# A gated attention block on one core: the first batch's second FFN matrix quantised in four pieces between the RELU low halves

## The reference, cut to what matters

```python
xn  = layernorm(x)
q, k, v = (gelu(xn @ W1n + b1n) @ W2n + b2n for n in "qkv")
s   = tril(q @ k.T / sqrt(C * T)) @ v          # scores times mask, no softmax
s   = layernorm(s) * ln_w + ln_b

def quantize(W):                                # to -1, 0, 1
    gamma = mean(abs(W))
    return clip(round(W / (gamma + 1e-5)), -1, 1)
h   = relu(xn @ quantize(W1).T + b1)            # 512 x 1024 for a batch
g   = silu(h @ quantize(W2).T + b2)
out = x + s * g
```

## Time and profile before

| | |
|---|---|
| median of the timed runs | 321.74 us |
| the profiled execution's own time | 322.64 us |
| its span | 320.8 us |
| mean granted PE clock | 0.983 |
| PE busy | 307.9 us (96%) |
| DVE busy | 242.2 us (75%) |
| ACT busy | 230.1 us (72%) |
| POOL busy | 129.8 us (40%) |

### The profile page before, as it was taken

How to read it: one execution, slowest core, us unless ns; L and a number is a source line. 1 busy time by engine, 2 the same in 40 slices (tenths; PEclk the granted TensorE clock), 3 DMA queues, 4 the chain that set the end, 5 groups by cost and what they waited for, 6 DMA issues and landing times.

```text
span 320.8 us, 5759 instructions
## 1 busy us (share of the span) xinstructions
PE 307.9 (96%) x1850; PEld 274.5 (86%) x1850; DVE 242.2 (75%) x556; ACT 230.1 (72%) x424; POOL 129.8 (40%) x106
## 2 busy tenths in 40 slices
PE   5998599999999999999999999999999999999993
PEld 5885499888998899888998899988998889988993
DVE  3589967797768887597787887597777977677677
ACT  1799553899549983799549984699648985599642
POOL 2015462526253542718245342817334362610223
PEclk9899599999999999999999999999999999999999
DMA  7943351320003100140003100050003200010001
GB/s 243 379 125 108 134 145 51 109 90 0 3 0 131 65 0 0 54 143 0 0 0 131 66 0 0 2 169 26 0 0 128 69 0 0 0 65 3 0 2 66
DMA packets 15771, 20.10 MB, mean 63 GB/s; under 512 B 1936, under 2 KB 12688, under 8 KB 15760
## 3 DMA queue, kind: packets, MB, share of 16 engines
q1 hardware_dynamic: 15056, 19.04, 17.7%
q10 hardware_dynamic: 704, 0.93, 0.8%
HBM read 15.74 MB, written 4.22 MB: 62 GB/s over the span
## 4 chain that ended last, share of the span: by engine, by line
PE 87%; DVE 5%; ACT 4%; DMA 2%; issue 1%; SPq 0%; DVEq 0%; ACTq 0%
PE bank L714 87%; DMA raw_qkv<-in_W2k 2%; ACT bank L367 1%; ACT g_hi L366 1%; DVE w2q L503 1%; DVE gw L584 1%; ACT r_lo L333 1%; DVE s L500 0%; DVE s_lo L614 0%; DVE x_stats L454 0%; ACT L366 0%; ACT o_square L340 0%; DVE s L604 0%; DVE x_all L639 0%; PE bank L699 0%
## 5 line engine op out<-in xcount | busy, mean ns | idle before, releaser
L557 DVE TENSOR_TENSOR r_lo<-bank,r_hi 128x512 fp32r<-128x512 f32 x64 | 42.5, 688 | 16.6 <-ACT bank L378 16.6
L377 ACT ACTIVATE r_hi<-bank,col 128x512 fp32r<-128x512 f32 x64 | 48.2, 754 | 0.0
L378 ACT ACTIVATE bank<-bank,col 128x512 f32<-128x512 f32 x64 | 46.9, 733 | 0.0
L296 POOL TENSOR_TENSOR y<-y,row 128x512 f32<-128x512 f32 x15 | 19.6, 1305 | 54.9 <-DVE gw L584 54.9
L714 PE MATMUL bank<-xT_lo,w1q 128*128 128x512 f32 x128 | 39.9, 393 | 0.1
L714 PE MATMUL bank<-xT_hi,w1q 128*128 128x512 f32 x128 | 39.8, 392 | 0.0
L280 POOL TENSOR_TENSOR y<-y,xn 128x512 f32<-128x512 f32 x14 | 23.6, 1683 | 37.3 <-DMA xn<-x_norm_rows 37.3
L289 POOL TENSOR_TENSOR v_lo<-v,v_hi 128x1024 fp32r<-128x1024 f32 x8 | 19.2, 2397 | 47.4 <-ACT v_hi L388 47.4
L392 ACT ACTIVATE y<-y 128x512 f32<-128x512 f32 (+1 forms) x17 | 10.3, 607 | 36.5 <-DVE y L575 36.5
L714 PE MATMUL bank<-w2q,r_lo 128*128 128x256 f32 x256 | 35.4, 281 | 0.0
L366 ACT ACTIVATE g_hi<-bank,col 128x512 fp32r<-128x512 f32 x48 | 33.2, 691 | 2.4 <-PE bank L714 2.3
(11 more groups left out here) (123 smaller groups left out, 703.9 us busy)
## 6 DMA issues: line engine op xcount, KB each, us to landing
out<-x_all SPq DMA_DIRECT2D x15, 256.0 KB, 2.6
x_all<-in_x SPq DMA_DIRECT2D x7, 512.0 KB, 3.6
y<-in_x_t SPq DMA_DIRECT2D x7, 512.0 KB, 3.4
xn<-x_norm_rows SPq DMA_DIRECT2D x7, 512.0 KB, 3.6
x_all<-in_w1t SPq DMA_DIRECT2D x1, 1024.0 KB, 8.1
x_all<-in_w2t SPq DMA_DIRECT2D x1, 1024.0 KB, 12.0
row<-in_rows ACTq DMA_DIRECT2D x1, 512.0 KB, 6.8
x_all<-in_x SPq DMA_DIRECT2D x1, 256.0 KB, 3.1
```

The lines of the kernel that those rows point to most:

```text
L296: nc.gpsimd.tensor_tensor(y[:, part], y[:, part], row[:, ROW_LNB:ROW_LNB + 1].broadcast_to((P, tiles, C)), ALU.mult).then_inc(gb_part, 1)
L377: nc.scalar.activation(r["hi"][:, f], pre[:], ACT.Relu, bias=b1)
L378: nc.scalar.activation(pre[:], pre[:], ACT.Relu, bias=b1).then_inc(f1_whole, 1)
L557: nc.vector.tensor_tensor(r["lo"][:, f], bank[(AT_F1 + f) % BANKS][:], r["hi"][:, f].bitcast(FP32), ALU.subtract).then_inc(r_split, 1)
```

## The change

The second matrix is quantised in four pieces of 128x512. `quantise` becomes a helper for one piece, `quantise1` does the first matrix in its two halves as before, and `quantise2(q)` does piece q of the second. In batch 0 the loop over the RELU low halves calls `quantise2` behind low halves 1, 3, 5 and 7. The pieces use the two halves of `flags` in turn. `w2_quantized` now counts to 4, for PE ahead of Y0 and for SyncE ahead of the loads of batches 4 to 7. The thresholds stay where they were.

```diff
-            sp.wait_ge(w2_quantized, 2)
+            sp.wait_ge(w2_quantized, 4)
...
+            def quantise(n, raw, quant, scratch, done, flagged):
+
+                nc.vector.tensor_scalar(scratch, raw, neg_thr[:, n:n + 1], None, ALU.is_lt).then_inc(flags_made, 1)
+                dve.wait_ge(flags_made, flagged)
+                nc.vector.scalar_tensor_tensor(quant, raw, thr[:, n:n + 1], scratch,
+                                               ALU.is_gt, ALU.subtract).then_inc(done, 1)
...
+            def quantise2(q):
+
+                part, scratch = slice(q * T, (q + 1) * T), flags[:, (q % 2) * T:(q % 2 + 1) * T]
+                if q > 1:
+                    dve.wait_ge(w2_quantized, q - 1)
+                quantise(1, raw2[:, part], w2q[:].rearrange("p a b -> p (a b)")[:, part], scratch,
+                         w2_quantized, q + 3)
...
                 if first:
                     thresholds(1, GAMMA[1])
-                    quantise(1, raw2, w2q[:].rearrange("p a b -> p (a b)"), w2_quantized)
+                    dve.wait_ge(thr_made, 4)
+                    dve.wait_ge(w1_quantized, 2)
                 for f in range(FT):
                     dve.wait_ge(f1_whole, 8 * i + f + 1)
                     nc.vector.tensor_tensor(r["lo"][:, f], bank[(AT_F1 + f) % BANKS][:], r["hi"][:, f].bitcast(FP32),
                                             ALU.subtract).then_inc(r_split, 1)
+                    if first and f % 2:
+                        quantise2(f // 2)
...
                 if first:
-                    pe.wait_ge(w2_quantized, 2)
+                    pe.wait_ge(w2_quantized, 4)
                 ffn_out(i, AT_Y0, (0, 1))
```

More of the change, by code:

```diff
@@ L491, in thresholds, with quantise1 @@
                                         ALU.mult, ALU.add).then_inc(thr_made, 1)
-            def quantise(n, raw, quant, done):
-                dve.wait_ge(thr_made, 2 * n + 2)
+            def quantise(n, raw, quant, scratch, done, flagged):
[3 more added lines that the diff above has]
+                                               ALU.is_gt, ALU.subtract).then_inc(done, 1)
+            def quantise1():
+                dve.wait_ge(thr_made, 2)
                 for h in range(2):
                     part = slice(h * F, (h + 1) * F)
[L498 to L504, removed]
+                    if h:
+                        dve.wait_ge(w1_quantized, 1)
+                    quantise(0, raw1[:, part], w1q[:].rearrange("p a b -> p (a b)")[:, part], flags,
+                             w1_quantized, h + 1)
+            def quantise2(q):
[4 more added lines that the diff above has]
+                         w2_quantized, q + 3)
             dve.wait_ge(fold_hi_made, 1)
@@ L512, in _ @@
             thresholds(0, GAMMA[0])
-            quantise(0, raw1, w1q[:].rearrange("p a b -> p (a b)"), w1_quantized)
+            quantise1()
             dve.wait_ge(folded, 2)
```

## The result

The changed kernel has a median of 323.44 us (322.14 to 325.84, 21 runs); the kernel before, in the same series, 320.96 us (320.12 to 323.73, 21 runs). The ratio is 1.0075, 95% interval 1.006 to 1.0091: slower by about 2.4 us (2.5 by the medians). The ratios are those of the runs within 1.5% of the fastest of their kernel, here all of them. The forecast was 324.4 against 321.74, a ratio of 1.008, in the range 319.0 to 325.2.

The account below looks back on a forecast made before the run. PE bounds the kernel, standing 3.73 us ahead of K for VectorE's quantising of the second FFN matrix. 322.64 + 0.63 (later Y0) + 2.0 (clock) = 325.3, or 324.4 on the timed median's scale; range 319.0 to 325.2.

Parts of the forecast that it names:

- The wait ahead of K goes: PE in batch 0: its 3.73 us wait ahead of K disappears, and K starts directly behind the w1q groups.
- A piece costs 1.14 us plain: VectorE, undisturbed: comparison 0.42 and second operation 0.75 us, with gap and overlap 1.14 per piece, 4.56 for four.
- Pieces 2 and 3 are stopped twice each: VectorE beside GpSimd's four operations on y: both operations of each piece wait for GpSimd; chance 0.50.
- rival B: Pieces 2 and 3 on VectorE are stopped only once each; net -0.6 to +0.7 us, 321.1 to 322.4; chance 0.28.
- rival A: VectorE's pieces are not stopped at all; Y0 3.77 us earlier, 318.0 to 320.3, middle 319.2; chance 0.22.
- Y0 0.63 us later: PE in batch 0: Y0, waiting for the last piece of w2q, starts at 44.42, 0.63 us later than before.
- The clock costs 2.0 us: PE under Y0: after standing 6.6 us it works at the lower clock, costing 2.0 us (ends 1.6 and 2.37).
- Nothing else becomes late: SyncE's x loads some 9.6 us later, GpSimd 1.0 and z_lo, v and x^T low halves about 5 cost nothing.

Follow-up runs that it names:

- the last experiment: The two halves kernel with batch 0's split of e moved from ahead of the quantising to behind the fifth RELU low half; 318.94 us, ratio 0.9943 to the kernel before.
- matmuls in the wait: The changed kernel with 16 extra 128x512 matmuls between D and Y0 in batch 0; 321.75 us, ratio 1.0027 to the kernel before.
- GpSimd held: The changed kernel, but GpSimd begins its four operations on y only when all four pieces of w2q are done; ratio 0.996 to the kernel before.
- two halves: The kernel before with its own 128x1024 halves, the second moved behind the second RELU low half; 317.5 us, ratio 0.989 to the kernel before.
- flags in a bank: The changed kernel with the flags of pieces 2 and 3 in Y0's PSUM bank instead of SBUF; 319.17 us, ratio 0.9931 to the kernel before.
- F1 repeated: The kernel before with the last F1 fill of batch 0 computed three times over; 320.98 us, ratio 0.9969 to the kernel before.

## Why the prediction was right

- **The wait ahead of K goes.** As said: K at 30.94 directly behind F1, and Y0's last conditions the only thing late. PE's wait there was 4.36 us and not the 6.6 forecast, since F1 itself ended late at a lower clock and Y0 came earlier.
- **A piece costs 1.14 us plain.** It was 1.19: the comparison took 0.48, between the 0.42 I took and 0.75. Worth some 0.2 us in four pieces.
- **Pieces 2 and 3 are stopped twice each.** Right in every step of the order: comparison, GpSimd, second operation, GpSimd, and the same again. Forecast recorded lengths 1.7, 2.1, 0.7 and 2.2; measured 1.29, 1.99, 0.54 and 1.89. Holding GpSimd gave back 3.25 us of the 3.25 that the records exceed their plain lengths (0.81 + 1.24 + 0.06 + 1.14). The two forms of the prediction's rival B (stopped once per piece) and rival A are refuted by the profile; that both kinds of operation are stopped, which the trace of before did not show for the comparison, the cast in the last experiment shows a second time.
- **Y0 0.63 us later.** The term that was off by most: it came 0.36 us earlier on the same scale. GpSimd had begun 0.58 us before piece 2's comparison and not 0.12 us (34.03 against 34.61), because it started 5.38 us after the first r_lo's start instead of 5.74. Each stop ends with GpSimd's operation, so an earlier GpSimd makes the first one shorter. That is 0.36 of the 0.99 us between forecast and profile. Another 0.51 is that GpSimd's last three operations ended 1.48, 1.39 and 1.37 us after VectorE had let them in, where I had put their whole recorded lengths, 1.53, 1.57 and 1.65. GpSimd's start moves from 5.34 to 5.84 us behind the first row of A in the profiles of this study; in the one with matmuls in the wait it was 5.80, and the same pieces gave + 0.25 and not - 0.36: which side of zero this term lies on depends on the execution.
- **The clock costs 2.0 us.** It fell in the wait as said, and cost 2.67 us in the profile; the matmuls in the wait gave back 2.4 there and 1.7 in the medians. This error and the last one largely cancel: 0.63 + 2.0 = 2.63 forecast, -0.36 + 2.6 = 2.2 in the profiles, 2.4 in the runs. So the mechanism was right, and that the sum came out this near was partly luck. There is more luck in the scale: both terms were counted from one execution of the kernel before, of a mean granted clock of 0.983. In 29 runs of it, taken beside four of the experiments (GpSimd held, two halves, flags in a bank, matmuls in the wait), only 8 had 0.983, and 14 had 0.993 or 0.994, while 17 of 21 of the changed kernel had 0.980 to 0.983.
- **Nothing else becomes late.** SyncE's four loads of x were issued from 41.94 to 53.3 and its next work is at 60.55; B is 277.0 to 277.2, as before, in the three rows of the table in which the clock stayed up from F1 on and GpSimd was not held (matmuls in the wait, F1 repeated, two halves).

The Trainium skill's page "SBUF — State Buffer", section "Who interferes with whom", has the rule: a VectorE instruction in a two-port mode, and one with two SBUF inputs beside a GpSimd instruction that reads SBUF, share a pair of ports with GpSimd as an exclusive lock, and whoever is second waits fully. The runs agree, for the comparison and the cast as for the operations with two SBUF inputs, with 0.13 to 0.21 us between the release and GpSimd's recorded end.

## What to carry to other kernels

Before work is moved on VectorE, look at what GpSimd does at the new place. Here an instruction that reads two SBUF tensors, or goes from SBUF to SBUF at double rate, ran alternately with GpSimd's of 128x512, and each of a pair that depend on each other waited for a whole GpSimd operation or what was left of it; with the flags in PSUM both ran free, for 0.28 us more in the comparison. A wait of PE that is moved can also bring its low clock to the new place: the 3.73 us ahead of K had it in the profile of before, the 4.36 ahead of Y0 in that of the changed kernel. I can give no length below which a wait is safe. The clock stayed up across 2.48 and 1.87 us, and fell in 3.07 and behind 2.42 and 1.01 with D between them, but of the six profiles with a wait of 1.54 or 1.55 us ahead of `abs_sum`, it fell a little later in two (the changed kernel and the one with GpSimd held) and stayed up in four.

## What the hardware showed that I had not expected

- When both engines always have the next operation ready, they alternate one for one: neither kept its place for the following instruction, though VectorE's came within 0.04 us.
- A GpSimd operation that was held is recorded longer by its wait (1.97, 2.05 and 2.12 us; those with no stopping instruction beside them 1.52 to 1.74), not later, so its start in the timeline is not the start of its work.
- The clock fell once at the start of the program in some executions and not in others (0.60 between 12 and 16 us, 1.00 in the profile of the changed kernel), and batch 0's FFN started 1.8 us apart. Absolute times of two profiles can't be compared across that. Distances within batch 0 are better, though not fixed either: A differed by 0.6 us between two kernels with the same VectorE program.
